# Where the modulation rows, the staged weights and the FFN scales travel in an adaLN layer on eight cores

## What is computed

```python
mod = (_silu(c) @ wmod).reshape(8, 6, 1, 1024)
sa, ca, ga, sb, cb, gb = (mod[:, k] for k in range(6))
ga = (2 * (ga >= 0) - 1) * jnp.maximum(jnp.abs(ga), 0.25)
gb = (2 * (gb >= 0) - 1) * jnp.maximum(jnp.abs(gb), 0.25)
h = _layernorm(x) * (1 + ca) + sa
# attention without softmax, 16 heads of 64:
q, k = relu(h @ Wq.T) / 8, relu(h @ Wk.T) / 8
v, u = h @ Wv.T, silu(h @ Wu.T)
kv  = k.T @ v                       # per head, over all tokens
x   = x + ga * ((_srms_norm(q @ kv) * u) @ Wo.T)
h   = _layernorm(x) * (1 + cb) + sb
# FFN: weight and tokens rounded to 127 steps with a scale each
w_q, w_scale = _quantize_per_channel(weight)
x_q, x_scale = _quantize_per_token(h)
x = x + gb * ((x_q @ w_q.T) * x_scale * w_scale.T + bias)
```

## Time and profile before

| | us |
|---|---|
| median of 3 runs | 492.27 |
| lowest, highest | 490.2, 528.13 |
| the profiled execution, its own time | 486.76 |
| its span on the slowest core (core 5) | 484.3 |
| spans of all cores | 467.4 to 484.3 |
| PE busy, DVE busy, ACT busy (core 5) | 397.9, 279.1, 231.4 |

### The profile page before, as it was taken

One profiled execution on the slowest core, in us unless ns is written; L12 is line 12 of the kernel. 1 busy time (PEld: TensorE's weight loads), 2 busy tenths in 40 slices (PEclk: granted clock), 3 DMA queues, 4 the chain that ended last, 5 costly groups with the idle time before them and its releaser, 6 DMA issues.

```text
span 484.3 us, 6412 instructions; the slowest of 8 cores (467.4 to 484.3 us)
## 1 busy us (share of the span) xinstructions
PE 397.9 (82%) x2052; PEld 185.2 (38%) x2052; DVE 279.1 (58%) x492; ACT 231.4 (48%) x327; POOL 80.8 (17%) x136
## 2 busy tenths in 40 slices
PE   3234499999999982878978199989999989998994
PEld 0121244455454440324433044434344434444441
DVE  3565751647206656478557256556476645765885
ACT  4342153764662310776486253374844467643431
POOL 3222310515000000000022002121122122022321
PEclk9985789999999995989999789998999999999999
DMA  7999899593996999979999605634526554265787
GB/s 224 272 279 278 212 203 294 220 292 127 231 244 203 320 301 271 204 213 387 355 110 125 162 0 88 131 67 108 87 65 122 120 88 104 72 130 89 92 140 158
DMA packets 21185, 87.03 MB, mean 180 GB/s; under 512 B 4257, under 2 KB 4257, under 8 KB 16290
## 3 DMA queue, kind: packets, MB, share of 16 engines
q1 hardware_dynamic: 13666, 58.33, 39.5%
q0 software_dynamic: 7488, 28.31, 34.4%
HBM read 70.36 MB, written 24.67 MB: 196 GB/s over the span
## 4 chain that ended last, share of the span: by engine, by line
PE 38%; DMA 30%; DVE 11%; ACT 9%; issue 8%; SPq 2%; POOL 1%; DVEq 0%; ACTq 0%; POOLq 0%
PE pb L360 33%; DMA rows<-ws_c 7%; DMA wa<-wmod_a 7%; DMA stage<-wmod_b 5%; DMA row_g<-rows 5%; DMA xr<-x_tm 4%; DVE stage L427 3%; SPq L46 2%; ACT rn L677 2%; ACT osq L667 2%; PE pb L386 2%; PE pb L675 1%; ACT xq L777 1%; DVE wm_c L485 1%; DMA silr<-rows 1%
## 5 line engine op out<-in xcount | busy, mean ns | idle before, releaser
L360 PE MATMUL pb<-wo_s,u_s 128*128 128x512 bf16 x256 | 62.5, 398 | 1.4 <-DVE u_s L657 1.4
L360 PE MATMUL pb<-fq,xqT 128*128 128x512 bf16 x256 | 60.1, 379 | 2.6 <-ACT xqT L789 2.3
L360 PE MATMUL pb<-h,wq_s 128*128 128x512 bf16 x256 | 61.6, 385 | 0.0
L360 PE MATMUL pb<-h,wu_s 128*128 128x512 bf16 x256 | 61.5, 386 | 0.0
L360 PE MATMUL pb<-wv_s,h 128*128 128x512 bf16 x256 | 58.5, 379 | 0.0
L360 PE MATMUL pb<-wk_s,h 128*128 128x512 bf16 x208 | 45.7, 379 | 0.0
L427 DVE SCALAR_TENSOR_TENSOR stage<-stage,silr 128x1024 f32<-128x1024 f32 x32 | 37.6, 1222 | 11.6 <-DMA stage<-wmod_b 11.6
L682 DVE SCALAR_TENSOR_TENSOR q_s<-rn,pb 128x512 bf16<-128x512 f32 x32 | 21.9, 687 | 37.5 <-ACT rn L680 37.1
L360 PEld LDWEIGHTS pb<-wo_s,u_s 128*128 128x128 bf16 x256 | 25.9, 102 | 34.2 <-issue 7.7
L360 PEld LDWEIGHTS pb<-h,wq_s 128*128 128x128 bf16 x256 | 25.3, 99 | 29.6 <-issue 1.9
L360 PEld LDWEIGHTS pb<-h,wu_s 128*128 128x128 bf16 x256 | 25.1, 99 | 29.0 <-issue 1.4
(11 more groups left out here) (91 smaller groups left out, 551.9 us busy)
## 6 DMA issues: line engine op xcount, KB each, us to landing
stage<-wmod_b SPq DMA_DIRECT2D x16, 1024.0 KB, 9.0
xr<-x_tm SPq DMA_DIRECT2D x21, 512.0 KB, 5.3
wa<-wmod_a SPq DMA_DIRECT2D x8, 1024.0 KB, 31.2
out_tm<-row_gbb SPq DMA_DIRECT2D x4, 2048.0 KB, 29.0
out_tm<-xr POOLq DMA_DIRECT2D x15, 512.0 KB, 8.3
out_tm<-h POOLq DMA_DIRECT2D x15, 512.0 KB, 5.6
xr<-x_tm POOLq DMA_DIRECT2D x8, 512.0 KB, 17.2
stage<-wo SPq DMA_DIRECT2D x4, 1024.0 KB, 17.8
```

Of the source, the lines that this page charges most:

```text
L360: t = PE.do(lambda e, dc=dc: e.matmul(pb[bank][:], lhs(dc), rhs(dc), start=(dc == 0), stop=(dc == NC - 1)), *after, each(dc) if each else ...
```

## The change

1. `put` and `get` are issued from POOL in place of SP. They no longer stand in `mod_fin` and between pieces but at fixed places (`row`): ga's after the stats of tile 15, sb's and cb's behind the two halves of Wq's load, gb's and gb*bias's behind Wu's load, which is now issued right behind the others.
2. `mod()` is called in every unit of `vproj(0)` and `vproj(1)` and in the first four of `kproj(2)`. The order of the pieces becomes ga, sb, cb, Wo, gb. `xhat` of tiles 12 to 15 moves from units 0-3 to units 4-7 of `kproj(2)`, the transposes of group 3 from units 0-3 to 2-5 of `vproj(2)`.
3. The FFN scales are turned by a PE matmul with an f32 identity (`id_f`, a new DVE copy in the prologue) into 8 rows of 128, copied by DVE and written to DRAM as 8 runs of 512 bytes, from POOL; before they went from SP in runs of 4 bytes.
4. `ffn_quant` runs in units 5-12 of group 0 in place of 6-13.
5. A one-element Ln on ACT (`warm`) stands behind the last `vproj`.

```diff
     def put(k, col, *after):
-        order = [[NC, 128], [1, NC]] if k < 5 else [[1, 128], [128, NC]]
-        put_tok[k] = SP.dma(sl_p[k], bass.AP(d_rows, k * D, order), col[:], *after, scattered=k > 4)
+        put_tok[k] = POOL.dma(sl_p[k], bass.AP(d_rows, k * D, [[NC, 128], [1, NC]]), col[:], *after)
     def get(k, row, *after):
-        row_tok[k] = SP.dma(sl_g[k], row[:], bass.AP(d_rows, k * D, [[0, 128], [1, D]]),
-                            put_tok[k], *after)
+        row_tok[k] = POOL.dma(sl_g[k], row[:], bass.AP(d_rows, k * D, [[0, 128], [1, D]]),
+                              put_tok[k], *after)
...
+    def row(v, dst, *after):
+        put(v, mod_c[v], col_tok[v])
+        get(v, dst, *after)
...
-    mods[8:8] = [lambda c=c: wo_piece(c) for c in range(4)]
+    mods[12:12] = [lambda c=c: wo_piece(c) for c in range(4)]
...
     for n, (hf, j) in enumerate(eight):
         vproj(1, hf, j)
...
         if n < 4:
             transp(2, n)
             stats(12 + n)
-        else:
-            mod()
+        if n == 3:
+            row(0, row_g)
+        mod()
+    load_w("wq", wq, 0, wa_free[NC - 1])
+    row(1, row_sb)
+    load_w("wq", wq, 1)
+    row(2, row_cb)
     for h in range(2):
-        load_w("wq", wq, h, wa_free[NC - 1])
+        load_w("wu", wu, h)
     for n, (hf, j) in enumerate(eight):
         kproj(2, hf, j)
...
         if n < 4:
-            xhat(12 + n)
-        mod()
+            mod()
+        else:
+            xhat(8 + n)
+    row(3, row_g, fold_tok[0])
+    put(4, gbb_c, col_tok[3])
+    get(4, row_gbb)
     for n, (hf, j) in enumerate(eight):
         vproj(2, hf, j)
...
-        if n < 4:
-            transp(3, n)
-        mod()
-    for h in range(2):
-        load_w("wu", wu, h, wa_free[NC - 1], st_tok[AT["gb"] + 3])
+        if 1 < n < 6:
+            transp(3, n - 2)
...
+    ACT.do(lambda e: e.activation(out=warm[:], in_=halfc, func=AF.Ln), t_half)
...
     def last_row():
-        put(5, ws_c, fw_tok[NC - 1])
+        t = PE.do(lambda e: e.matmul(pb[7][0:NC, 0:128], ws_c[:], id_f[:], start=True, stop=True),
+                  fw_tok[NC - 1], t_idf, b7[0])
+        b7[0] = t = DVE.do(lambda e: e.tensor_copy(out=ws_t[:], in_=pb[7][0:NC, 0:128]), t)
+        put_tok[5] = POOL.dma(sl_p[5], bass.AP(d_rows, 5 * D, [[128, NC], [1, 128]]), ws_t[:], t)
         get(5, silr, col_tok[3])
...
     for n in range(16):
         xunit(0, n)
-        if fquant and n > 5:
-            fquant.pop(0)()
+        if 4 < n < 13:
+            ffn_quant(n - 5)
         if n > 7:
             ffn_transp(n - 8)
```

More of the change, by code:

```diff
@@ L38, in do, with dma @@
         return (self.sem, self.n)
-    def dma(self, slot, out, in_, *after, add=False, scattered=False):
+    def dma(self, slot, out, in_, *after, add=False):
         slot.n += 16
         how = {"accum_op": ALU.add} if add else {}
-        if scattered:
-            how["allow_slow_non_contiguous"] = True
         self.items.append(([t for t in after if t is not None],
@@ L145, in build_nc @@
     mod_c = [sb(f"mod_c{v}", [128, NC]) for v in range(4)]
+    id_f = sb("id_f", [128, 128])
+    ws_t = sb("ws_t", [NC, 128])
+    warm = sb("warm", [128, 1])
     sgn_c = sb("sgn_c", [128, NC])
@@ L240, in build_nc @@
     wa_free = {}
-    stream = ([(d_wb, (0 * NC + 2 * c) * D, 4 * NC * D) for c in range(4)]
-              + [(d_wb, (1 * NC + 2 * c) * D, 4 * NC * D) for c in range(4)]
+    stream = ([(d_wb, (v * NC + 2 * c) * D, 4 * NC * D) for v in range(3) for c in range(4)]
               + [(d_wo, 2 * c * D, NC * D) for c in range(4)]
-              + [(d_wb, (2 * NC + 2 * c) * D, 4 * NC * D) for c in range(4)]
               + [(d_wb, (3 * NC + 2 * c) * D, 4 * NC * D) for c in range(4)]
               + [(d_fw, 2 * c * D, NC * D) for c in range(4)])
-    AT = {"ga": 0, "sb": 4, "wo": 8, "cb": 12, "gb": 16, "ffn": 20}
+    AT = {"ga": 0, "sb": 4, "cb": 8, "wo": 12, "gb": 16, "ffn": 20}
     def load_stage(n, *after):
@@ L456, in mod_fin @@
                                                         op0=ALU.subtract, op1=ALU.mult), t)
-        put(v, m, t)
         if v == 3:
@@ L460, in mod_fin @@
                        t, t_const)
-            put(4, gbb_c, t)
-            get(3, row_g, fold_tok[0])
-            get(4, row_gbb)
-    ROWS = {0: row_g, 1: row_sb, 2: row_cb}
+        col_tok[v] = t
+    def row(v, dst, *after):
+        put(v, mod_c[v], col_tok[v])
+        get(v, dst, *after)
     def wo_piece(c):
@@ L542, in build_nc @@
             transp(1, dc - 4)
+    t_idf = DVE.do(lambda e: e.tensor_copy(out=id_f[:], in_=id_b[:]), t_const)
     def more_x(g):
@@ L558, in piece @@
         mod_piece(v, c)
-        if c == 2 and v:
-            get(v - 1, ROWS[v - 1])
         if c == 3:
@@ L619, in build_nc @@
             kvprod(2, 3)
-    fquant = [lambda ec=ec: ffn_quant(ec) for ec in range(NC)]
     for n, (hf, j) in enumerate(eight):
```

3 lines of the change are left out of this document (1 added, 2 removed).

## The result

| | before | changed |
|---|---|---|
| first comparison: median of 4 runs each, us | 503.99 | 474.71 |
| lowest, highest | 490.2, 528.13 | 472.23, 476.05 |
| ratio, with its 95% interval | | 0.966 [0.958, 0.974] |
| second comparison, another chip: medians | 487.15 | 474.20 |
| ratio, with its 95% interval | | 0.972 [0.968, 0.976] |

The change makes the kernel faster, by 3.4% in the first comparison and 2.8% in the second. The forecast, 472.0 against 492.27, was 4.1%.

What follows compares the result with a forecast made beforehand. PE bounds the kernel, with two stalls a change of transfers can win. Terms sum to -17.5 us (486.8 to 469.3); core 1 becomes slowest at 470.0, plus 2 gives 472, range 461 to 484.

Steps and rivals of the forecast that it cites:

- 1, second stall: PE's stall while DVE waits for the scales' row at `gws` goes, the write leaving the fills' queue: -9.0 us.
- 2, its cold matmuls: Behind the second stall, two groups of eight matmuls no longer run at PE's lower clock: -2.5 us.
- 3, first stall: Before the first `ohead`: ga's row earlier relative to the pieces, gb done 4 us sooner; -4.0 us, ends -10.1 and +10.
- 4, `warm`: The Ln table load leaves the first head's chain for where ACT is idle: -1.3 us, ends -1.5 and 0.
- 5, quantising earlier: PE's waits for `wi` before six transposes of FFN weights shrink: -2.5 us, ends -3.5 and +1.
- 6, scales' matmul: Behind the last transposes PE waits for ACT to empty bank 7, then runs one matmul: +1.8 us.
- rival (d): On POOL's serial queue, write landings cost 12.5 us each, delaying Wu and `norm1`: 497 us, chance 0.09.
- rival (c): At `gws`: scales' row still late as fills and x tiles fill the engines: 483.5 us, chance 0.09.
- The hidden wait on POOL: `norm1` of tile 0 behind the scales' write: 3 us taken for a write, 6.9 us hidden, so no cost.
- (a): At the first stall: pieces keep coming at some 3 us each and it goes whole: 466 us, chance 0.20.
- (b): Before the first `ohead`: Wq and Wu loads hold gb's pieces back, stall stays or grows: 476 to 484 us, chance 0.12.

Runs made afterwards that it cites:

- experiment 7: The changed kernel without the one-element Ln `warm`: 473.16 us against 493.02 for the kernel before.
- experiment 6: The changed kernel with `ffn_quant` back in units 6 to 13: 475.69 us against 493.02 for the kernel before.
- experiment 1: The changed kernel with the FFN scales' write and row read issued from SP again, in runs of 512 bytes: 469.4 us against 493.02 before.
- experiment 4: The kernel before with only the PE turn of the scales, write and row still from SP: 480.19 us against 490.88 before.
- experiment 3: The kernel before with only the PE turn of the scales, write and row from POOL: 479.36 us against 490.88 before.
- experiment 10: The changed kernel with both halves of Wq and Wu issued ahead of sb's and cb's rows: 482.53 us against 487.15 before.

## Why the prediction was right or wrong

The forecast of 472.0 us lies 2.7 below the first comparison's median and 2.2 below the second's, and faster by over 2% came true. Term by term, on core 5, whose span went from 484.3 to 469.8:

| term | forecast | measured on core 5 | seen in |
|---|---|---|---|
| 1, second stall | -9.0 | -9.0 | `gws` without a wait |
| 2, its cold matmuls (at the lower clock) | -2.5 | -2.5 | the clock at 9 in these slices of core 5 |
| 3, first stall | -4.0 | -4.1 | first `ohead` 190.70 to 186.58 |
| 4, `warm` | -1.3 | -1.2 | experiment 7 |
| 5, quantising earlier | -2.5 | -0.5 | experiment 6 |
| 6, scales' matmul | +1.8 | +1.9 | 2.32 less 0.44 from transposes to the next projection |
| POOL's wait before `norm1` | 0 | +2.3 | from L860 to the fourth `ohead` 20.19, median of experiment 1 17.9 |
| cold matmuls behind the first stall | not counted | -1.4 | 3.24 to 1.89 us for eight |
| sum | -17.5 | -14.5 | |

The sum can be checked by three stretches of the same core: to the first `ohead` -4.1; from there to the last transposes 44.1 to 40.8 us, -3.4 (terms 4, 5 and the cold matmuls: -3.1); from there to the end 249.5 to 242.5, -7.0 (the other terms: -7.3). The parts fit the whole to 0.3 us, which is better than they are known: experiment 1's own stretch from the next projection to the fourth `ohead` is 0.6 us longer than before's (17.55 in the median against 16.95 on core 5), half of it the `shead`'s wait of 2.22 for 1.95. The forecast was 3 us too good on this core.

**The step that failed in its reason** is the one of the second stall: "The write goes to POOL's queue, away from the fills". The size was right, the cause wrong. I had read the 34.73 us as the price of standing behind 8 MB in one queue, and weighed only what another queue would bring ("the write's landing" in rival (d) and the 25 us of cover in rival (c) are of the same kind; nowhere did I price the 1024 runs, though the diff does away with them). Experiment 2 has the new queue and keeps the runs of 4 bytes: the write takes 25.6 us and the kernel 489. Experiments 1 and 4 keep the queue and change the runs: no stall on any core. The diff's third part was thus not a detail beside the queue but the part that works. The comparison by which I decided was not a fair one: 11.2 us for POOL's transfers of large runs says nothing of 1024 small ones.

The queue has a price of its own, which was hidden. In the fills' queue the write of 8 runs is through 21 to 26 us behind the issue of the last fill on every core of experiments 1 and 4, whether it was itself issued 3 us behind the fills or 12; with 1024 runs, before, it was 31 to 42 us. On POOL's queue it takes 7.0 to 8.7 us in the changed kernel and 5.5 to 7.8 in experiment 3, where the fills' queue takes 9.6 to 21.7 from the write's issue to the read's. But nothing waits for the difference. The rule of the Trainium skill that I weighed against the new queue ("DMA: Bandwidth & Descriptors", Issuing engines are not separate DMA queues) is borne out in so far as the write with 1024 runs was still late from POOL, and the fills with it. For the write in 8 runs it is not: that one is through sooner from POOL, 5.5 to 7.8 us against 11.7 to 18.6 (experiments 3 and 4).

**Term 5 was mis-sized**, by 2.0 us. I counted the waits that end (five on this core in before, 2.55 us together, not six) and said only "DVE's work is the same". Moved one unit earlier, that work lands in front of a head's scaling, and PE waits 1.39 us there. And the waits for `wi` had left room for a group of matmuls at the lower clock. Without them the group behind the second transposes costs 1.2 us, on this core and on two of three in all (experiment 6).

**The hidden wait on POOL** was mis-sized. 3 us were taken for a write, with 12.5 as the other end and 6.9 hidden. It was 8.1 us on core 5 and 8.7 on core 2, so 1.2 to 1.8 over the cover; PE lost 2.3 and 2.8 against experiment 1's median. On core 5 the wait itself is 1.6 of it (1.88 against 0.24). The eight matmuls behind were at the lower clock on seven of eight cores in experiment 1 too, so that loss is not the wait's, though they took 3.62 us here and 3.05 to 3.52 there. Before it was so on one core only (core 6, 3.11 us); no run tells what brought it. Rival (d) was this mechanism at a larger price. Its other half, Wu late for U, did not come: Wu was issued at 177.3 against 178.5 in the working. The single writes of sb and cb waited 11.2 and 20.9 us, but on the half of Wq that I had counted apart.

**Term 3** had the right size by luck, by two errors that cancelled. The row of ga did not come at 143 but at 147.6, as late as before: tile 15's statistics were on time (131.6, forecast 131.7), but POOL's three small instructions of that tile lasted to 136.4, so the write was issued at 136.6, not 134.5; it took 4.2 us in place of 3 and the row 6.2 in place of 5.4. The five pieces then needed 32.6 us to 180.2, not 37, and gb was done at 182.7, forecast 184. The idle time before the first `ohead` is 2.9 us, not the 5 to 6 that I named, because the last `kvprod` came at 179.6 on this core (176.5 before); DVE, not PE, sets that start. Before, six of eight cores had a first stall over 1 us (1.2 to 10.1), now four have (1.2 to 2.9). Group 3's transposes, said to be just in time, waited 0.9 and 1.3 us on two cores.

**The slowest core.** I took core 1 for it with a span of 467.5, and it was 467.0. But cores 2, 5 and 7 were slower. Core 2 had little to win, a second stall of 2.43 us and no first one; now it has a first stall of 2.88, and the longest of the new waits, 2.40. So it rose from 467.4 to 470.7. In the profiled execution of the second comparison the slowest was core 3, and in the others of it cores 3, 4, 5 and 6. Which core is the slowest changes from one execution to the next, so that a sum for one core tends to lie below the slowest of eight.

Of the rivals, (a) and (c) were not seen, and (b) only in experiment 10. With the runs of 4 bytes left in (experiment 2) it is (d)'s mechanism that comes, `norm1` behind the write on POOL, at 25.6 us for the write. The lower end of the range, 461, does not follow from what it is said to be: (a)'s 466 with term 5 at its best is 465.
